# Four-layer graph network: GpSimd takes part of layer 0's last products, and pass 1's closing is written in fewer operations

## The chip, the cores and the metric

The kernel runs on one core of a Trainium2 chip. The metric is the device time in microseconds, the median over several executions. One further execution was recorded by the hardware profiler; all rows below are from it.

## The reference, cut to what matters

```python
edge_index = stack([src, dst])                       # 100000 edges sorted by dst, 6250 nodes, 256 features
x = layernorm(x + L0(x, edge_index))                 # GAT, 8 heads of 32
x = layernorm(x + L1(x, edge_index))                 # two GCN convolutions, 256 -> 512 -> 256
x = layernorm(x + L2(x, edge_weight, src, dst))
x = layernorm(x + L3(x, edge_index, edge_attr_2))
...
# L0, for each edge: the row of its source times a weight for each head, summed over dst
e = leaky_relu(a_src[src] + a_dst[dst], 0.2); e_exp = exp(e - e_max[dst])
out = segment_sum(h[src] * e_exp[:, :, None]) / denom; out = relu(out + bias)
...
# L1
h = relu(layer_norm(gcn_conv(x, W1, b1), gamma1, beta1))   # layer_norm: (h - mu) * rsqrt(var + eps) * gamma + beta
g = relu(layer_norm(gcn_conv(h, W2, b2), gamma2, beta2))
```

## The kernel before

The 6250 nodes lie in 49 tiles of 128. The edges, sorted by destination, are worked through in steps of at most 128 edges of one tile. For each step GpSimd starts an indirect DMA that gathers the source rows, TensorE multiplies them by a one-hot matrix of destinations, and VectorE adds the product to the tile's sums (`reg_acc`). When a tile has all its steps, its closing follows, spread over the steps behind: `closing(i)` in layer 0 and `closings(i)` in the passes say which tile is in which part `n` at step `i`. All orders are written out by hand, engine by engine, and each engine works its program in order. A wait is a `wait_ge` on a semaphore.

**Layer 0** (`heads_*`) has 832 steps in 52 groups of 16; the groups 50 and 51 are the last. `heads_gpsimd` issues the 832 gathers (L1031), then waits for all of them and copies the shifted edge indices into `src_idx` (L1037) for the passes. A gathered row must be multiplied by its eight weights before TensorE can use it. `heads_vector` does that for step `i` ("weigh", L1354), then a part of the next group's scores (`chain_vector`), then `add(i - 3)` (L1337), then the part of the closing. The weights of a group come from ScalarE (L1114) at the end of the group before, after VectorE's `below` (L1276). The wait in `add` for the add before it makes adds follow one another. TensorE waits for `weighted0(i)` in order of `i`. L943 to L972 are a tile's closing on VectorE, L992 to L1000 that on ScalarE. Afterwards the last normed tile is stored, and GpSimd begins pass 1.

**Pass 1** is the first half of L1 and what lies between its two convolutions, 783 gathers. `pass1_vector` closes a tile in these parts: scale and bias out of PSUM (L1563, n = 5), moments (L1567, L1569), reciprocal of the root, subtract and scale (L1572, L1574, n = 8), gamma (L1577), beta (L1580). `pass1_scalar` makes the root (L1539), the relu (L1543, n = 11), and the copies of turned tiles out of PSUM (`Dense.keep`, L165; TensorE's `turn` and `multiply` are L157 and L172). GpSimd begins pass 2 (`e.wait_ge(*h2_stored.end)`) when the last tile's result (L1548) is stored. Passes 2 and 3 are built alike. In pass 2, L1714 and L1722 are gamma and beta over 256 columns. L2114 and L2130, in layer 3's closing, are an addition on GpSimd and a multiplication on VectorE over seven tiles at once.

Of the kernel before, what the change touches and what calls it, by code (L numbers as in the profile page):

```python
# [13 lines left out]
P = 128  # L14
# [125 lines left out]
class Dense:  # L140
# [20 lines left out]
    def keep(self, e, j):  # L161
        e.wait_ge(*self.turned(j))
        if j >= 2:
            e.wait_ge(*self.product(j - 2))
        e.copy(self.ring[:, j % 2, :], self.turn_bank(j)[:, 0:self.k_chunks * P]).then_inc(*self.kept.up)  # L165
# [94 lines left out]
def build(nc, io):  # L260
    ctx = ExitStack()
    with ctx:
# [84 lines left out]
        s_chain = {n: signal(f"{n}_chain") for n in ("vector", "tensor", "scalar")}  # L347
        s_far, s_hot4 = signal("distance_made"), signal("four_hots_made")
# [3 lines left out]
        s_cleared, s_hidden = signal("sums_cleared"), signal("hidden_made")  # L352
# [659 lines left out]
        weighted0 = s_weighted.take(STEPS_PAD)  # L1012
        product0, added0 = s_edge.take(STEPS_PAD), s_added.take(STEPS_PAD)
        scaled0, denscaled0 = s_scaled.take(GROUPS - 1), s_denscaled.take(GROUPS - 1)

# [6 lines left out]
        def heads_gpsimd(e):  # L1022
# [11 lines left out]
            for k in range(3):  # L1034
                e.wait_ge(*got0[k].end)
            e.wait_ge(*h0_v.at("src_at"))
# [280 lines left out]
        def heads_vector(e):  # L1317
# [31 lines left out]
            for i in range(STEPS_PAD):  # L1349
                g, k = i // S, i % S  # L1350
                row = rows0[:, i % (3 * S), :]
                v = row[:, 0:FEAT].rearrange("p (h d) -> p h d", h=H)
                e.wait_ge(*ch_a.at("weights", g))
                e.tensor_tensor(v, v, bcast(row[:, FEAT:ROW0], 2, [P, H, D]), ALU.mult).then_inc(*weighted0.up)  # L1354
# [125 lines left out]
        def closings(i):  # L1480
# [16 lines left out]
        stat1, moment1, inverse1, shift1, gamma1_done, beta1_done = (  # L1497
            s.take(NODE_TILES) for s in (norm_a[0], norm_a[1], norm_a[3], norm_a[4], s_gamma, s_beta))
        root1, hidden = s_hid_in.take(NODE_TILES), s_hidden.take(NODE_TILES)
# [13 lines left out]
        def pass1_tensor(e):  # L1513
            e.wait_ge(*loads1.end)
            for i in range(RANKED + PARTS):
                if i < RANKED:
                    edges1.step(e, i)
                for k, n in closings(i):
# [3 lines left out]
                    if n == 4:  # L1522
                        dense1.multiply(e, k, taken1)
                    if n == 12:
                        e.wait_ge(*hidden(k))
                        dense2.turn(e, k)
                    if n == 14:
                        dense2.multiply(e, k, taken2)

        def pass1_scalar(e):  # L1530
            edges1.hots(e, range(8))
            for i in range(RANKED + PARTS):
                edges1.hots_ahead(e, i)
                for k, n in closings(i):
# [5 lines left out]
                    if n == 11:  # L1540
                        h = hid[:, k % 4, :]
                        e.wait_ge(*beta1_done(k))
                        e.activation(h, h, ACT.Relu).then_inc(*hidden.up)  # L1543
                    if n == 13:
                        dense2.keep(e, k)
                    if n == 16:
# [719 lines left out]
```

## Time and profile before

| | |
|---|---|
| median of 3 runs | 5286.16 us (5281.18 to 5288.01) |
| profiled execution | 5284.91 us, its span 5283.1 us |
| TensorE's granted clock, mean | 0.824 of full speed |
| busy in the span | PE 74%, VectorE (DVE) 66%, ScalarE (ACT) 49%, GpSimd (POOL) 73% |
| layer 0's steps | to about 1209 us |
| pass 1, pass 2, pass 3, layer 3 | from 1216, 2226, 3223 and 4213 us |

The span runs from the first to the last instruction. Busy shares are means over stages with different limits.

### The profile page before, as it was taken

The numbers are of one execution on the slowest core, as the hardware profiler recorded it, in microseconds if no ns is written. First come the engines' busy times: TensorE is split into PE (matmuls) and PEld (weight loads), VectorE is DVE, ScalarE is ACT, GpSimd is POOL, SyncE is SP. The second block draws the span as 40 slices with busy tenths as digits, with TensorE's granted clock in tenths as the row PEclk, the third lists the DMA queues.
The fourth block names the chain that finished last, engine by engine and source line by source line (L and its number), as shares of the span: only waits on it lengthen the run. The fifth ranks groups of instructions, "written<-read, shape, count | busy, mean of one in ns | idle before, by whom it ended". The sixth has DMA issues, their size and how long they took to land.

```text
span 5283.1 us, 86663 instructions
## 1 busy us (share of the span) xinstructions
PE 3888.6 (74%) x13357; PEld 2393.2 (45%) x13357; DVE 3504.2 (66%) x10780; ACT 2567.7 (49%) x6941; POOL 3861.1 (73%) x3995
## 2 busy tenths in 40 slices
PE   7888888886777777677777777676777657666663
PEld 5666666663444444344434434343334334444442
DVE  5889888885555455354444445666666578888887
ACT  3667666674555555355555551000000166666665
POOL 3777777766777777677777776777777777777775
PEclk8889889898998999777787787878887777777776
DMA  6444444433333333443333333333333322222222
GB/s 171 117 123 123 123 122 122 124 108 106 110 112 111 112 111 112 127 133 112 113 112 111 112 112 100 109 109 109 109 110 109 97 57 57 57 57 57 57 57 67
DMA packets 252627, 549.14 MB, mean 104 GB/s; under 512 B 71467, under 2 KB 136235, under 8 KB 252108
## 3 DMA queue, kind: packets, MB, share of 16 engines
q0 software_dynamic: 178752, 478.34, 33.3%
q1 hardware_dynamic: 45804, 42.37, 2.6%
q10 hardware_dynamic: 27552, 22.89, 1.5%
q8 instruction: 157, 2.57, 0.2%
q14 instruction: 362, 2.97, 0.2%
HBM read 501.16 MB, written 42.15 MB: 103 GB/s over the span
## 4 chain that ended last, share of the span: by engine, by line
POOL 55%; issue 20%; PE 10%; ACT 6%; DVE 4%; DMA 2%; SPq 1%; DVEq 0%; ACTq 0%; POOLq 0%
POOL scratch L1416 41%; POOL scratch L1886 14%; PE bank L1312 5%; PE bank L1161 3%; ACT scratch L1073 2%; DMA scratch<-tab_x,src_idx 1%; DVE reg_acc L1337 1%; PE bank L1149 1%; ACT scratch L1085 1%; DVE reg_x L1354 1%; SPq L872 1%; ACT scratch L1076 1%; DMA scratch<-tab_h,src_idx 1%; POOL reg_x L1031 0%; ACT scratch L1121 0%
## 5 line engine op out<-in xcount | busy, mean ns | idle before, releaser
L1468 PE MATMUL bank<-scratch 128*128 x4986 | 1904.2, 495 | 761.6 <-SPq L1428 407.3
L1478 DVE TENSOR_TENSOR reg_acc<-reg_acc,bank 128x256 f32 x2493 | 1048.1, 420 | 1361.7 <-PE bank L1468 1298.4
L1416 POOL DMA_INDIRECT scratch<-tab_x,src_idx x1566 | 1491.5, 952 | 533.3 <-issue 469.4
L1468 PEld LDWEIGHTS bank<-scratch 128*128 128x128 f32 x4986 | 964.3, 228 | 1602.9 <-issue 1549.0
L1031 POOL DMA_INDIRECT reg_x<-tab_h,src_idx x832 | 831.6, 1000 | 291.0 <-issue 176.7
L1416 POOL DMA_INDIRECT scratch<-tab_h,src_idx x783 | 744.4, 951 | 260.7 <-issue 234.3
L1886 POOL DMA_INDIRECT scratch<-tab_h,src_idx x783 | 741.2, 947 | 248.6 <-issue 237.7
L1937 PE MATMUL bank<-reg_w,scratch 128*128 128x260 f32 x1664 | 637.5, 527 | 286.6 <-issue 185.2
L1437 ACT ACTIVATE scratch<-iota_row,dst_loc 128x128 f32<-128x128 f32 x1662 | 572.1, 392 | 348.2 <-PE bank L1468 333.9
L1312 PE MATMUL bank<-reg_x,scratch 128*128 128x265 f32 x1664 | 577.8, 458 | 73.3 <-DVE reg_x L1354 71.1
L1937 PEld LDWEIGHTS bank<-reg_w,scratch 128*128 128x128 f32 x1664 | 377.3, 253 | 509.7 <-issue 312.1
L1968 ACT ACTIVATE edge_w<-scratch,attr 128x68 f32 x832 | 288.5, 347 | 311.1 <-SPq L1898 281.9
L1312 PEld LDWEIGHTS bank<-reg_x,scratch 128*128 128x128 f32 x1664 | 302.9, 215 | 203.6 <-DVE reg_x L1354 172.1
L1337 DVE TENSOR_TENSOR reg_acc<-reg_acc,bank 128x265 f32 x832 | 355.3, 427 | 45.8 <-PE bank L1312 35.3
L2054 DVE TENSOR_TENSOR reg_acc<-reg_acc,bank 128x260 f32 x832 | 350.3, 421 | 16.1 <-PE bank L1937 3.6
L1354 DVE TENSOR_TENSOR reg_x<-reg_x 128x256 f32<-128x256 f32 x832 | 344.6, 414 | 0.5 <-ACT reg_x L1114 0.5
L1453 DVE TENSOR_SCALAR scratch<-iota_row,dst_loc,edge_w 128x128 f32<-128x128 f32 x831 | 322.3, 389 | 6.1 <-issue 6.1
L1952 ACT ACTIVATE scratch<-iota_row,dst_loc 128x128 f32<-128x128 f32 x832 | 319.8, 386 | 3.4 <-DMA tab_h<-reg_w 1.6
L1787 ACT ACTIVATE adst<-adst,small 128x1 f32<-128x1 f32 x49 | 14.4, 294 | 611.2 <-DVE adst L1830 611.2
L2037 DVE SCALAR_TENSOR_TENSOR reg_w<-scratch,attr,edge_w 128x68 f32<-128x68 f32 x832 | 237.8, 286 | 95.0 <-ACT edge_w L1968 83.4
L2085 DVE TENSOR_TENSOR reg_w<-reg_w,bank 128x520 f32<-128x520 f32 x416 | 286.2, 688 | 0.5
L1442 ACT ACTIVATE scratch<-scratch 128x512 f32<-128x512 f32 x416 | 261.7, 629 | 13.1
(314 smaller groups left out, 4374.9 us busy)
## 6 DMA issues: line engine op xcount, KB each, us to landing
scratch<-tab_x,src_idx POOLq DMA_INDIRECT x1566, 2.8
scratch<-tab_h,src_idx POOLq DMA_INDIRECT x1566, 2.7
reg_x<-tab_h,src_idx POOLq DMA_INDIRECT x832
tab_h<-scratch ACTq DMA_DIRECT2D x7, 924.0 KB, 6.4
reg_x<-in_x SPq DMA_DIRECT2D x7, 896.0 KB, 11.3
reg_w<-in_x SPq DMA_DIRECT2D x49, 128.0 KB, 2.5
tab_x<-reg_acc SPq DMA_DIRECT2D x49, 128.0 KB
tab_xs<-reg_w SPq DMA_DIRECT2D x49, 128.0 KB, 2.7
```

Of the source, the lines that this page charges most:

```text
L1031: e.indirect_dma_start(rows0[:, t % (3 * S), 0:ROW0], None, tab_h0, bass.IndirectOffsetOnAxis(ap=src_idx[:, t:t + 1], axis=0)).then_inc(*g ...
L1312: e.matmul(psum[i % BANKS0][:, 0:W0_ROW], hots0[:, i % (2 * S), :], rows0[:, i % (3 * S), :], start=True, stop=True).then_inc(*product0.up)
L1337: e.tensor_tensor(v, v, psum[i % BANKS0][:, 0:W0_ROW], ALU.add).then_inc(*added0.up)
L1354: e.tensor_tensor(v, v, bcast(row[:, FEAT:ROW0], 2, [P, H, D]), ALU.mult).then_inc(*weighted0.up)
L1416: e.indirect_dma_start(ring_rows[:, j % SLOTS, :], None, self.table, bass.IndirectOffsetOnAxis(ap=src_idx[:, j:j + 1], axis=0)).then_inc(* ...
L1437: e.activation(ring_hots[:, i % HOTS, :], iota_row[:, :], ACT.Abs, scale=-1.0, bias=dst_loc[:, i:i + 1]).then_inc(*self.far.up)
L1453: e.tensor_scalar(ring_hots[:, i % HOTS, :], iota_row[:, :], dst_loc[:, i:i + 1], edge_w[:, i:i + 1], ALU.is_equal, ALU.mult).then_inc(*se ...
L1468: e.matmul(self.bank(i), ring_hots[:, i % HOTS, :], rows, start=True, stop=True).then_inc(*self.product.up)
L1478: e.tensor_tensor(v, v, self.bank(i), ALU.add).then_inc(*self.added.up)
L1886: e.indirect_dma_start(ring_rows[:, j % SLOTS, 0:ROW3], None, tab_h3, bass.IndirectOffsetOnAxis(ap=src_idx[:, j:j + 1], axis=0)).then_inc( ...
L1937: e.matmul(psum[i % BANKS][:, 0:WIDE3], hots3[:, i % HOTS, :], scaled3[:, i % 4, :], start=True, stop=True).then_inc(*product3.up)
L2054: e.tensor_tensor(v, v, psum[i % BANKS][:, 0:WIDE3], ALU.add).then_inc(*added3.up)
```

## The change

In layer 0, `BY_POOL` holds the even steps of the last two groups, 16 steps. GpSimd multiplies their rows, behind its last gather and ahead of the copy of `src_idx`; VectorE skips them. In pass 1, (h - mean) * gamma is one `scalar_tensor_tensor`, made beside the root, and (that) * inverse + beta a second one; the relu is taken in the activation that copies the turned tile out of PSUM. `keep` is an `activation` everywhere now, with the function Copy by default.

```diff
-    def keep(self, e, j):
+    def keep(self, e, j, act=ACT.Copy):
...
-        e.copy(self.ring[:, j % 2, :], self.turn_bank(j)[:, 0:self.k_chunks * P]).then_inc(*self.kept.up)
+        e.activation(self.ring[:, j % 2, :], self.turn_bank(j)[:, 0:self.k_chunks * P], act).then_inc(*self.kept.up)
...
-        weighted0 = s_weighted.take(STEPS_PAD)
+        BY_POOL = [i for i in range(STEPS_PAD - 2 * S, STEPS_PAD) if i % 2 == 0]
+        weighted_v = s_weighted.take(STEPS_PAD - len(BY_POOL))
+        weighted_p = s_pool_weighted.take(len(BY_POOL))
...
+        def weighted0(i):
+            return weighted_p(BY_POOL.index(i)) if i in BY_POOL else weighted_v(i - sum(n < i for n in BY_POOL))
+
+        def weigh(e, i):
+            row = rows0[:, i % (3 * S), :]
+            v = row[:, 0:FEAT].rearrange("p (h d) -> p h d", h=H)
+            return e.tensor_tensor(v, v, bcast(row[:, FEAT:ROW0], 2, [P, H, D]), ALU.mult)
...
             for k in range(3):
                 e.wait_ge(*got0[k].end)
+            for i in BY_POOL:
+                e.wait_ge(*ch_a.at("weights", i // S))
+                weigh(e, i).then_inc(*weighted_p.up)
             e.wait_ge(*h0_v.at("src_at"))
             e.tensor_copy(src_idx[:, 0:POSITIONS], src_at_i).then_inc(*h0_p.done("src_idx"))
...
-                e.wait_ge(*ch_a.at("weights", g))
-                e.tensor_tensor(v, v, bcast(row[:, FEAT:ROW0], 2, [P, H, D]), ALU.mult).then_inc(*weighted0.up)
+                if i not in BY_POOL:
+                    e.wait_ge(*ch_a.at("weights", g))
+                    weigh(e, i).then_inc(*weighted_v.up)
...
-                    if n == 12:
-                        e.wait_ge(*hidden(k))
-                        dense2.turn(e, k)
-                    if n == 14:
+                    if n == 10:
+                        e.wait_ge(*beta1_done(k))
+                        dense2.turn(e, k)
+                    if n == 12:
                         dense2.multiply(e, k, taken2)
...
                     if n == 11:
-                        h = hid[:, k % 4, :]
-                        e.wait_ge(*beta1_done(k))
-                        e.activation(h, h, ACT.Relu).then_inc(*hidden.up)
-                    if n == 13:
-                        dense2.keep(e, k)
-                    if n == 16:
+                        dense2.keep(e, k, ACT.Relu)
+                    if n == 14:
...
+                    if n == 7:
+                        e.wait_ge(*moment1(k))
+                        e.scalar_tensor_tensor(out=h, in0=h, scalar=cells_a.mean(k), in1=gamma1, op0=ALU.subtract,
+                                               op1=ALU.mult).then_inc(*gamma1_done.up)
                     if n == 8:
                         e.wait_ge(*root1(k))
                         e.reciprocal(root, root).then_inc(*inverse1.up)
+                    if n == 9:
                         e.wait_ge(*inverse1(k))
-                        e.tensor_scalar(h, h, cells_a.mean(k), root, ALU.subtract, ALU.mult).then_inc(*shift1.up)
-                    if n == 9:
-                        e.wait_ge(*shift1(k))
-                        e.tensor_tensor(h, h, gamma1, ALU.mult).then_inc(*gamma1_done.up)
-                    if n == 10:
                         e.wait_ge(*gamma1_done(k))
-                        e.tensor_tensor(h, h, beta1, ALU.add).then_inc(*beta1_done.up)
+                        e.scalar_tensor_tensor(out=h, in0=h, scalar=root, in1=beta1, op0=ALU.mult,
+                                               op1=ALU.add).then_inc(*beta1_done.up)
```

The order of GpSimd's instructions behind layer 0's gathers, before:

```order
L1031 DMA reg_x<-tab_h,src_idx 128x264 x832
L1037 COPY src_idx<-reg_w 128x783
L1416 DMA scratch<-tab_x,src_idx 128x256 x783
L1416 DMA scratch<-tab_h,src_idx 128x256 x783
L1416 DMA scratch<-tab_x,src_idx 128x256 x783
L1886 DMA scratch<-tab_h,src_idx 128x136 x783
```

and of the change:

```order
L1042 DMA reg_x<-tab_h,src_idx 128x264 x832
L1025 TENSOR_TENSOR reg_x<-reg_x 128x256 x16
L1051 COPY src_idx<-reg_w 128x783
L1429 DMA scratch<-tab_x,src_idx 128x256 x783
L1429 DMA scratch<-tab_h,src_idx 128x256 x783
L1429 DMA scratch<-tab_x,src_idx 128x256 x783
```

The sixteen multiplications stand between the gathers of layer 0 and the copy.

VectorE amid group 51, before (L1354 is a weigh, L1337 an add, L962 and L966 are the closing of a tile; ISA is a wait):

```order
L1337 TENSOR_TENSOR reg_acc<-reg_acc,bank 128x265
L962 SCALAR_TENSOR_TENSOR reg_w<-reg_acc,reg_w 128x256
L1354 TENSOR_TENSOR reg_x<-reg_x 128x256
L877 ISA
L1337 TENSOR_TENSOR reg_acc<-reg_acc,bank 128x265
L966 BN_STATS small<-reg_w 128x6
L1354 TENSOR_TENSOR reg_x<-reg_x 128x256
L877 ISA
L1337 TENSOR_TENSOR reg_acc<-reg_acc,bank 128x265
```

and of the change, where L1025 is a weigh and L1351 an add:

```order
L1351 TENSOR_TENSOR reg_acc<-reg_acc,bank 128x265
L963 SCALAR_TENSOR_TENSOR reg_w<-reg_acc,reg_w 128x256
L1025 TENSOR_TENSOR reg_x<-reg_x 128x256
L878 ISA
L1351 TENSOR_TENSOR reg_acc<-reg_acc,bank 128x265
L967 BN_STATS small<-reg_w 128x6
L878 ISA
L1351 TENSOR_TENSOR reg_acc<-reg_acc,bank 128x265
L970 BN_AGGR small<-small 128x2
```

Between stats and the add behind them the weigh is gone.

VectorE at the last tile's closing in pass 1, before (`adst` holds the moments and the root, `reg_x` the hidden rows, `reg_w` bias, gamma and beta):

```order
L1563 SCALAR_TENSOR_TENSOR reg_x<-bank,dinv,reg_w 128x512
L1567 BN_STATS adst<-reg_x 128x6
L1569 BN_AGGR adst<-adst 128x2
L1572 RECIPROCAL adst<-adst 128x1
L1574 TENSOR_SCALAR reg_x<-reg_x,adst 128x512
L1577 TENSOR_TENSOR reg_x<-reg_x,reg_w 128x512
L1580 TENSOR_TENSOR reg_x<-reg_x,reg_w 128x512
```

and of the change:

```order
L1572 SCALAR_TENSOR_TENSOR reg_x<-bank,dinv,reg_w 128x512
L1576 BN_STATS adst<-reg_x 128x6
L1578 BN_AGGR adst<-adst 128x2
L1581 SCALAR_TENSOR_TENSOR reg_x<-reg_x,adst,reg_w 128x512
L1585 RECIPROCAL adst<-adst 128x1
L1589 SCALAR_TENSOR_TENSOR reg_x<-reg_x,adst,reg_w 128x512
```

Gamma moved ahead of the reciprocal, and three wide operations behind the moments became two.

## Rows read from the trace of the kernel before

**Rows 1.** The page: the chain that ended last, by engine

```profile
POOL 55%; issue 20%; PE 10%; ACT 6%; DVE 4%; DMA 2%; SPq 1%; DVEq 0%; ACTq 0%; POOLq 0%
```

**Rows 2.** Busy us by stretch: length, PE, PEld, DVE, ACT, POOL, clock, DMA share, GB/s

```profile
1216.00:2203.00 987.00, 762.86 (x2514) 445.47 (x2515) 494.70 (x1163) 509.19 (x1276) 748.74 (x783) 0.91 0.39 113
```

**Rows 3.** Timeline of GpSimd: start, us, operation, [idle before, releaser]

```profile
1172.10 0.92 POOL L1037 COPY src_idx<-reg_w 128x783 int32<-128x783 int32 x1 [2.55 <-DMA reg_x<-tab_h,src_idx]
1216.02 0.98 POOL L1416 DMA_INDIRECT scratch<-tab_x,src_idx  x1 [43.01 <-DMA tab_x<-reg_acc]
```

**Rows 4.** Timeline of VectorE: one operation in groups 49 and 50

```profile
1172.23 0.81 DVE L1273 TENSOR_SCALAR scratch<-scratch 128x8 f32<-128x8 f32 x1
...
1191.45 0.17 DVE L1273 TENSOR_SCALAR scratch<-scratch 128x8 f32<-128x8 f32 x1
```

**Rows 5.** Timeline of VectorE in group 51

```profile
1199.46 0.42 DVE L966 BATCH_NORM_STATS2 small<-reg_w 128x6 f32<-128x256 f32 x1
1199.79 0.41 DVE L1354 TENSOR_TENSOR reg_x<-reg_x 128x256 f32<-128x256 f32 x1
...
1207.83 0.43 DVE L1337 TENSOR_TENSOR reg_acc<-reg_acc,bank 128x265 f32 x1 [0.22 <-DVE reg_acc L1337]
```

**Rows 6.** Timeline of ScalarE in group 50

```profile
1177.50 0.48 ACT L1121 COPY scratch<-bank 128x384 f32<-128x384 f32 x1 [1.12 <-PE bank L1170]
...
1186.89 0.16 ACT L1102 COPY scratch<-bank 128x2 f32<-128x2 f32 x1
...
1192.52 0.32 ACT L1114 ACTIVATE reg_x<-scratch 128x128 f32<-128x128 f32 x1 [2.92 <-DVE scratch L1276]
```

**Rows 7.** Timeline of GpSimd in layer 3's closing

```profile
5230.81 5.43 POOL L2114 TENSOR_TENSOR reg_x<-reg_acc,reg_x 128x1792 f32<-128x1792 f32 x1
...
5258.05 3.65 POOL L2114 TENSOR_TENSOR reg_x<-reg_acc,reg_x 128x1792 f32<-128x1792 f32 x1
```

**Rows 8.** Timeline of VectorE in layer 3's closing

```profile
5227.27 5.46 DVE L2130 TENSOR_TENSOR reg_acc<-reg_acc,edge_w 128x1792 f32<-128x1792 f32 x1
```

**Rows 9.** Timeline of GpSimd in pass 1, three of its longest gathers

```profile
1272.32 1.42 POOL L1416 DMA_INDIRECT scratch<-tab_x,src_idx  x1 [0.30 <-issue]
1291.56 1.37 POOL L1416 DMA_INDIRECT scratch<-tab_x,src_idx  x1 [0.30 <-issue]
...
2200.02 1.37 POOL L1416 DMA_INDIRECT scratch<-tab_x,src_idx  x1 [0.30 <-issue]
```

**Rows 10.** Timeline of VectorE beside the second of them

```profile
1291.42 0.68 DVE L1580 TENSOR_TENSOR reg_x<-reg_x,reg_w 128x512 f32<-128x512 f32 x1
```

**Rows 11.** The chain in order of time, tail of pass 1: start, us, what

```profile
2213.01 0.30 ACT adst L1539
...
2213.34 0.18 DVE adst L1572
...
2213.54 0.56 DVE reg_x L1574
...
2214.12 0.70 DVE reg_x L1577
...
2214.85 0.70 DVE reg_x L1580
...
2215.57 0.64 ACT reg_x L1543
...
2216.26 1.13 PE bank L157 x4
```

**Rows 12.** Groups of VectorE in pass 1 and pass 2: busy us, mean ns | idle before

```profile
L1563 DVE SCALAR_TENSOR_TENSOR reg_x<-bank,dinv,reg_w 128x512 f32<-128x512 f32 x49 | 36.5, 745 | 4.0 <-PE bank L172 4.0
...
L1714 DVE SCALAR_TENSOR_TENSOR reg_acc<-reg_acc,adst,reg_w 128x256 f32<-128x256 f32 x49 | 23.6, 481 | 0.0
```

**Rows 13.** Group of ScalarE in pass 1: the keep of 512 columns

```profile
L165 ACT COPY reg_x<-bank 128x512 f32<-128x512 f32 x49 | 28.3, 578 | 34.8 <-PE bank L157 34.7
```

**Rows 14.** The line of the gathers in pass 1: ns min, median, max

```profile
L1416 POOL DMA_INDIRECT scratch<-tab_x,src_idx x783: 942/946/1451, 1216.0 to 2202.9; - x196
```

More of the change, by code:

```diff
@@ L347, in build @@
         s_chain = {n: signal(f"{n}_chain") for n in ("vector", "tensor", "scalar")}
+        s_pool_weighted = signal("rows_weighted_by_gpsimd")
         s_far, s_hot4 = signal("distance_made"), signal("four_hots_made")
@@ L351, in build @@
         s_degree, s_gamma, s_beta = signal("degree_scaled"), signal("gamma_scaled"), signal("beta_added")
-        s_cleared, s_hidden = signal("sums_cleared"), signal("hidden_made")
+        s_cleared = signal("sums_cleared")
         s_hid_in, s_hid_v = signal("hidden_root"), signal("hidden_normed")
@@ L1350, in heads_vector @@
                 g, k = i // S, i % S
-                row = rows0[:, i % (3 * S), :]
-                v = row[:, 0:FEAT].rearrange("p (h d) -> p h d", h=H)
-                e.wait_ge(*ch_a.at("weights", g))
-                e.tensor_tensor(v, v, bcast(row[:, FEAT:ROW0], 2, [P, H, D]), ALU.mult).then_inc(*weighted0.up)
+                if i not in BY_POOL:
+                    e.wait_ge(*ch_a.at("weights", g))
+                    weigh(e, i).then_inc(*weighted_v.up)
                 if g + 1 < GROUPS:
@@ L1496, in build @@
         taken1, taken2 = s_taken.take(NODE_TILES), s_taken2.take(NODE_TILES)
-        stat1, moment1, inverse1, shift1, gamma1_done, beta1_done = (
-            s.take(NODE_TILES) for s in (norm_a[0], norm_a[1], norm_a[3], norm_a[4], s_gamma, s_beta))
-        root1, hidden = s_hid_in.take(NODE_TILES), s_hidden.take(NODE_TILES)
+        stat1, moment1, inverse1, gamma1_done, beta1_done = (
+            s.take(NODE_TILES) for s in (norm_a[0], norm_a[1], norm_a[3], s_gamma, s_beta))
+        root1 = s_hid_in.take(NODE_TILES)
         h2_stored = s_store.take(T)
```

## The prediction

> **What bounds the kernel now.** I read the page's chain first. GpSimd has 55% of it and "issue" 20% [rows 1]. Both are one thing: GpSimd makes the descriptors of a gather in about 0.95 us and starts the next 0.30 us later. From 1216 to 2203 us GpSimd runs 783 gathers, 748.74 us busy, while PE, VectorE and ScalarE are at 77%, 50% and 52% [rows 2]. So in pass 1 work taken from VectorE or ScalarE is worth nothing as such. Only three kinds of place can move the end: where GpSimd has nothing to issue (before 1216 us it sat idle 43.01 us until the last tile of layer 0 was stored [rows 3]); the serial tail of pass 1 behind the last gather; and whatever makes one gather longer than its 0.95 us. The timeline was read next for the end of layer 0, then the chain for the tail, then the gathers' durations.
>
> **Part 1a, the tail of pass 1.** After the last gather one tile goes through its closing alone, and the chain names every step [rows 11]: root 2213.01 (0.30), reciprocal 2213.34 (0.18), subtract and scale 2213.54 (0.56), gamma 2214.12 (0.70), beta 2214.85 (0.70), relu 2215.57 (0.64), TensorE's turn at 2216.26. Pass 2's first gather waits for what follows. In the new order gamma comes first, needs only the moments, and so starts at 2213.01 beside the root. Its form, scalar_tensor_tensor with a pointer scalar over 512 columns, stands in the trace at 745 ns (its first input from PSUM), and at 256 columns with both inputs in SBUF at 481 ns [rows 12]. I take 0.745: done 2213.76. The root (0.30) is done by then. Reciprocal: in pass 2, whose code has this form already, it adds about 0.10 behind such an operation, so 2213.86. With 0.02 of hand-over the second fused operation runs 2213.88 to 2214.62, and the turn starts with 0.05 more at 2214.67, against 2216.26: **-1.6 us**. Bounds: -1.8 if each takes 0.68 like gamma and beta, -1.3 if the reciprocal waits its full 0.18 and each takes 0.80.
>
> **Part 1b, the copies.** Every dense keep was a COPY (578 ns at 512 columns [rows 13]) and is now an activation. The nearest activation of 512 columns is the relu that is removed, 0.64 in [rows 11]. Some 0.05 each; in serial places stand two in pass 1's tail and one in pass 3's: **+0.15 us** (0 to +0.3). The other keeps lie under the gathers.
>
> **Part 1c, the gathers of pass 1.** Against the median of 946 ns [rows 14], 748.74 us for 783 gathers is 8.0 us too much. The long ones come about once a tile; 42 lie above 0.97 us, the first and the last are in [rows 9]. The one of 1291.56 took 1.37 with beta, begun at 1291.42, over its start [rows 9, 10]. I set all 42 beside VectorE's timeline: 16 begin under beta (their excess over 0.95 adds up to 5.2 us), 15 under gamma (2.35), 11 under the subtract and scale (1.5). A gather that begins while such an operation runs ends as late as the operation lets it start; L1563, with one input in PSUM, never does that in 49 tiles. So two of the three culprits go or change: three operations become two, both with two SBUF inputs. Each fused one follows a step with little behind it, as gamma did in most tiles, while beta came on a backlog of three wide operations. I price each like gamma, raised by (0.56/0.50) squared for its longer hold: 2.9 us, together 5.9 against 9.0: **-3.1 us**. Bounds: -8 if no gather is hit any more, +4 if both fall like beta (2 x 5.2 x 1.25 = 13).
>
> The Trainium skill (SBUF — State Buffer, Who interferes with whom) has a VectorE instruction with two SBUF inputs contend with GpSimd instructions that read SBUF, and infers that a tensor_tensor leaves descriptor generation alone. The trace shows otherwise for beta, by the 1.37 us. By that inference all the excess would belong to the subtract and scale and would go.
>
> **Part 2, the end of layer 0.** Sixteen multiplications of 128x256 leave VectorE and go to GpSimd, behind its last gather and ahead of the copy of src_idx. VectorE paces these stretches, at one weigh and one add a step.
> - *The copy moves.* It ran at 1172.10 for 0.92 [rows 3] and VectorE's L1273, issued under it, took 0.81 instead of 0.17 [rows 4]; that is on the chain. Gone here: -0.64. It comes back behind the multiplications, amid group 51, and blocks one operation by up to 0.9: +0.4.
> - *Price of one multiplication on GpSimd.* Nearest rows: 128x1792 took 3.65 undisturbed, the last of its seven [rows 7]. With 0.1 fixed, 256 columns give 0.61, of which some 0.55 hold what VectorE also needs. That it is held exclusively, turn by turn, shows in layer 3's residual at the program's end: VectorE's multiplication issued at 5227.27 took 5.46 instead of 2.0, ended at 5232.7, and GpSimd's, begun at 5230.81, took 5.43 instead of 3.65 [rows 7, 8].
> - *Group 50.* ScalarE works without a gap that VectorE decides from 1177.50 to 1187.05 [rows 6], so eight weighs saved and eight turns lost there stay hidden: 0. Without that cover the eight blocks cost up to 8 x 0.3 = 2.4 less the 2.7 of the saved weighs. Only the weigh of step 814 stands between the last scores and the weights of group 51: -0.34.
> - *Group 51* (from 1192.84 [rows 6]). Before, a step was 0.67: weigh 0.34 and add 0.34. Two adds in a row cannot be nearer than 0.65, since each waits 0.22 for the last [rows 5]. A weigh that goes saves 0.33 only where another operation fills its place, as stats at 1199.46 in front of the weigh of 1199.79 [rows 5]: two such and three half ones, -1.0. Against it: a pair of steps needs VectorE's weigh after two of GpSimd's turns (2 x 0.55 + 0.05 + 0.34 = 1.49 instead of 1.34), four pairs: +0.6, and the five or six closing operations with two SBUF inputs wait some 0.3 each: +1.7. Net +1.3; with turns of 0.45, +0.6; with 1.0, +4.3.
> Sum: -0.64 + 0.4 - 0.34 + 1.3 = **+0.7 us**, bounds -1.5 and +6. GpSimd is done near 1200 us, long before 1216.02 [rows 3]. The first product of group 51 is not later than before: GpSimd starts it with the weights, while VectorE had an add in hand.
>
> **Sum.** -1.6 + 0.15 - 3.1 + 0.7 = -3.85 us. On the profiled execution's 5284.91 that is 5281.1; on the median of the three runs, 5286.16, it is **5282.3 us**. The profiled one lies 1.25 under the median, inside the runs' own spread of 6.8. A change of 0.2% (10.6 us) is about what a measurement of this kernel can tell from none. So the forecast is: no measurable change.
>
> **Rivals.**
> 1. *Gathers free (the skill's inference).* If only the subtract and scale held the gathers up, -8.0 replaces -3.1: 5277.4. Against it: [rows 9, 10], and 31 of 42. Chance 0.08.
> 2. *GpSimd's multiplication is dear.* Its operands here are 8 blocks of 32 columns with a broadcast factor, a shape that the trace lacks. At 1.0 us each, layer 0 loses 3.7 instead of 0.7: 5285.3. Chance 0.12.
> 3. *Slower.* The same mechanism at its far end: the eighth product of group 51 (row 830) is ready at 1192 + 8X, and its add stood at 1207.83 [rows 5], its matmul 1 us ahead. From X = 1.85 us on GpSimd paces the end. To lose 10.6 us over the whole it must cost 15.2 here: X = 3.75, about what the whole 128x1792 operation takes. 5296.8 or more. Chance 0.03.
> 4. *Faster by more than 0.2%.* All stalls gone (-8), the tail -1.8, layer 0 at its lower bound -1.5: -11.3, 5274.9. All three bounds at once: 0.05.
> 5. *Nothing from part 2.* The group-50 saving is hidden and group 51 even: 5281.6; not to be told from the forecast.
> The forecast with its own range (5278 to 5288) has 0.72.
>
> **Chances and range.** Rivals 1, 2 and the forecast lie within 0.2%: 0.92; faster 0.05; slower 0.03. The range takes rivals 1 and 2, the stall term's +4 and a spread of 3 us between runs: 5275 to 5290.
>
> **What would show it.** In the tail: gamma's row beside the root's, and some 1.6 us less from moments to turn. In pass 1: busy time of the 783 gathers near 746 us, no gather long under an operation with an input in PSUM. At 1172: L1273's successor at 0.17. In group 51: sixteen GpSimd rows of 0.6, the first eight within 10 us, VectorE's two-input rows stretched to 0.6 to 0.9, and the stretch from the weights to the last add some 1.3 longer. I would be wrong if the multiplications took over 1 us, if the stalls fell in a fixed bad phase (13 us or more), or if the hand-over of 1216 moved by more than 2 us either way.

## The result: 39 us slower, outside the predicted range

In alternating runs on one chip the changed kernel took 5326.63 us in the median (5326.12 to 5332.12), the kernel before 5287.09 (5281.18 to 5292.37): a ratio of **1.0077, with a 95% interval of 1.006 to 1.0095**. 5282.3 us had been predicted, 5275 to 5290.

The chain of the kernel after, by engine, reads as that of [rows 1] did, to the percent or nearly:

```profile
POOL 55%; issue 20%; PE 10%; ACT 5%; DVE 4%; DMA 3%; SPq 0%; DVEq 0%; ACTq 0%; POOLq 0%
```

No new wait and no new bound shows in it. The busy time of the engines in pass 1 of the kernel after (the columns are those of [rows 2]) says more:

```profile
1217.50:2221.00 1003.50, 764.69 (x2518) 448.11 (x2519) 474.14 (x1114) 489.61 (x1229) 764.93 (x783) 0.92 0.39 111
```

VectorE and ScalarE have 20 us less to do each, as meant. But the 783 gathers keep GpSimd busy for 764.93 us, against 748.74. The stretches of the profiled executions, from first gather to first gather and so on, give the whole difference (spans 5283.1 and 5324.4 us):

| stretch | before | after | difference |
|---|---|---|---|
| start to pass 1's first gather | 1216.0 | 1217.5 | +1.5 |
| pass 1, first to last gather | 986.9 | 1002.4 | +15.4 |
| tail of pass 1, to pass 2's first gather | 23.4 | 21.2 | -2.2 |
| pass 2, first to last gather | 981.7 | 991.0 | +9.4 |
| pass 3, the same | 979.2 | 987.7 | +8.5 |
| layer 3, the same | 978.5 | 987.1 | +8.6 |
| the two hand-overs between, and the end | 117.4 | 117.6 | +0.2 |

Passes 2 and 3 and layer 3 have not one changed instruction of GpSimd, and lose 26 us of the 41. The line of the gathers shows how: one stretch after another of the kernel after, duration in ns as minimum/median/maximum, then first and last start:

```profile
L1042 POOL DMA_INDIRECT reg_x<-tab_h,src_idx x832: 949/954/1686, 85.5 to 1171.7; - x167
L1429 POOL DMA_INDIRECT scratch<-tab_x,src_idx x783: 952/957/1482, 1217.5 to 2219.9; - x196
L1896 POOL DMA_INDIRECT scratch<-tab_h,src_idx x783: 951/955/1169, 4246.1 to 5233.2; - x196
```

and the first and the last of these lines in the kernel before (the middle one is in [rows 14], 942/946/1451):

```profile
L1031 POOL DMA_INDIRECT reg_x<-tab_h,src_idx x832: 942/947/2046, 84.7 to 1168.3; - x167
L1886 POOL DMA_INDIRECT scratch<-tab_h,src_idx x783: 938/944/1194, 4213.1 to 5191.7; - x196
```

The gathers have become 7 to 13 ns longer, in the minimum as well as in the median. That is 1% of a gather, and there are 3964 of them in layer 0, the passes and layer 3, issued back to back. It holds for layer 0's gathers too, which begin at 85 us, long before the first of the sixteen multiplications runs at 1174.79. Even the seven small gathers of the preparation (`reg_acc<-in_edge_floats`, from 30 us on) take 954 ns in the mean against 945. So it is no collision with what the change executes nearby. Three times 782 pitches that are 11 to 12 ns longer make the 26.5 us of the last three passes. In pass 1 the same 11 ns give 8.6 us of the 15.4; the other 6.7 or so are longer stalls, treated below.

What the sixteen multiplications cost GpSimd itself is as forecast. The timeline of GpSimd in the kernel after, behind its last gather of layer 0 (consecutive ones are joined, "x8"):

```profile
1174.79 5.86 POOL L1025 TENSOR_TENSOR reg_x<-reg_x 128x256 f32<-128x256 f32 x8 [2.08 <-DMA reg_x<-tab_h,src_idx]
1192.94 5.38 POOL L1025 TENSOR_TENSOR reg_x<-reg_x 128x256 f32<-128x256 f32 x8 [12.28 <-ACT reg_x L1128]
1198.27 1.03 POOL L1051 COPY src_idx<-reg_w 128x783 int32<-128x783 int32 x1
1217.52 1.02 POOL L1429 DMA_INDIRECT scratch<-tab_x,src_idx  x1 [18.22 <-DMA tab_x<-reg_acc]
```

and its line (minimum, median, maximum):

```profile
L1025 POOL TENSOR_TENSOR reg_x<-reg_x x16: 612/792/827, 1174.8 to 1197.5; 128x256 f32<-128x256 f32 x16
```

### The profile page after: what moved, and what is told of

The parts are those of the page before. It is cut to its first block, busy times and chain, and to the rows that moved or that the text cites. A ratio compares the mean times of both kernels' runs of the same rounds, so it can differ in the third digit from the quotient of the medians.

```text
span 5324.4 us, 86614 instructions
## 1 busy us (share of the span) xinstructions
PE 3917.3 (74%) x13357; PEld 2397.2 (45%) x13357; DVE 3474.2 (65%) x10715; ACT 2552.6 (48%) x6892; POOL 3915.5 (74%) x4011
## 4 chain that ended last, share of the span: by engine, by line
POOL 55%; issue 20%; PE 10%; ACT 5%; DVE 4%; DMA 3%; SPq 0%; DVEq 0%; ACTq 0%; POOLq 0%
POOL scratch L1429 41%; POOL scratch L1896 14%; PE bank L1326 5%; PE bank L1175 3%; ACT scratch L1087 2%; PE bank L1163 1%; DVE reg_acc L1351 1%; ACT scratch L1099 1%; DMA scratch<-tab_h,src_idx 1%; DMA reg_x<-tab_h,src_idx 1%; DMA scratch<-tab_x,src_idx 1%; DVE reg_x L1025 1%; POOL reg_x L1042 1%; ACT scratch L1090 1%; SPq L873 0%
## 5 line engine op out<-in xcount | busy, mean ns | idle before, releaser
L1429 POOL DMA_INDIRECT scratch<-tab_x,src_idx x1566 | 1515.2, 968 | 508.9 <-issue 472.8
L1429 POOL DMA_INDIRECT scratch<-tab_h,src_idx x783 | 753.6, 962 | 258.6 <-issue 235.3
L1896 POOL DMA_INDIRECT scratch<-tab_h,src_idx x783 | 749.8, 958 | 248.7 <-issue 236.4
L1351 DVE TENSOR_TENSOR reg_acc<-reg_acc,bank 128x265 f32 x832 | 353.1, 424 | 35.2 <-PE bank L1326 22.9
L1025 DVE TENSOR_TENSOR reg_x<-reg_x 128x256 f32<-128x256 f32 x816 | 337.0, 413 | 0.5 <-ACT reg_x L1128 0.5
L1466 DVE TENSOR_SCALAR scratch<-iota_row,dst_loc,edge_w 128x128 f32<-128x128 f32 x831 | 308.6, 372 | 6.1 <-issue 6.1
```

What stands on the lines that cost most here:

```text
L1025: return e.tensor_tensor(v, v, bcast(row[:, FEAT:ROW0], 2, [P, H, D]), ALU.mult)
L1351: e.tensor_tensor(v, v, psum[i % BANKS0][:, 0:W0_ROW], ALU.add).then_inc(*added0.up)
L1429: e.indirect_dma_start(ring_rows[:, j % SLOTS, :], None, self.table, bass.IndirectOffsetOnAxis(ap=src_idx[:, j:j + 1], axis=0)).then_inc(* ...
L1896: e.indirect_dma_start(ring_rows[:, j % SLOTS, 0:ROW3], None, tab_h3, bass.IndirectOffsetOnAxis(ap=src_idx[:, j:j + 1], axis=0)).then_inc( ...
```

## Experiments

**A remark on the chips.** The groups of runs fell on different chips, and on three of them the same kernel before takes 6669 to 6765 us: there GpSimd's gathers last as long as elsewhere but are not what bounds. The page of such a run (`e3_one_semaphore`, the kernel before but for one unused semaphore) has this chain, and this group of the gathers, before which GpSimd waited 463 us for SyncE's queue:

```profile
PE 43%; issue 26%; another core or an unknown queue 8%; DVE 8%; ACT 7%; DVEq 3%; ACTq 2%; SPq 1%; POOL 1%; DMA 0%; POOLq 0%
...
L1417 POOL DMA_INDIRECT scratch<-tab_x,src_idx x1566 | 1492.8, 953 | 1005.9 <-SPq L1427 463.2
```

So of those runs I use the durations of the gathers, which can be compared across chips, and their times only against the kernel before on the same chip.

| run | gathers, median ns | time, us | before there, us |
|---|---|---|---|
| e1_pass1_only | 946 | 6608.5, ratio 0.9876 [0.9852, 0.9901] | 6683.9 |
| e2_gpsimd_only | 960 | 6671.5, 0.9978 [0.9956, 1.0001] | 6683.9 |
| e3_one_semaphore | 946 | 6682.5, 1.0001 [0.9982, 1.0021] | 6683.9 |
| e4_after_again | 957 | 6596.7, 0.9859 [0.9819, 0.9899] | 6683.9 |
| e5_pass1_only_again | 946 | 5286.3, 1.0002 [0.9992, 1.0012] | 5283.5 |
| f1_one_product | 957 | 5326.1 | 5283.5 |
| f2_sixteen_memsets | 946 | 5280.0 | 5283.5 |
| f3_sixteen_plain | 957 | 5327.1 | 5283.5 |
| g1_sixteen_adds | 960 | 6666.5 | 6669.1 |
| g2_no_gpsimd_add | 946 | 6679.7, 1.002 [0.9998, 1.0041] | 6669.1 |
| g3_no_gpsimd_copy | 946 | 6670.1 | 6669.1 |
| g4_second_later | 949 | 6654.3, 0.997 [0.9946, 0.9995] | 6669.1 |
| h1_products_no_copy | 946 | 5297.8, 1.0001 [0.9987, 1.0015] | 5297.9 |
| h2_behind_copy | 946 | 5291.9 | 5297.9 |
| h3_behind_gathers | 949 | 5298.9 | 5297.9 |
| h4_after_moved | 960 | 5331.9 | 5297.9 |
| i1_copy_first | 957 | 6696.3, 0.9904 [0.988, 0.9929] | 6764.7 |
| i2_product_first | 946 | 6771.0 | 6764.7 |

Times without a ratio are single executions; those of the kernel before on one chip differ among themselves by up to 29 us (5287.4 to 5316.3 beside h1), so a single time can show the loss of 34 us or more that is at stake here, and nothing finer. The median is that of the passes' first line (passes 1 and 3). Two groups stand apart: 946 to 949, and 957 to 960.

### Which part of the change does it

Theory A: the work on GpSimd lengthens the gathers. Rival: the new semaphore, or pass 1's new order. The changed kernel without the multiplications:

```diff
-        BY_POOL = [i for i in range(STEPS_PAD - 2 * S, STEPS_PAD) if i % 2 == 0]
+        BY_POOL = []
```

> The changed kernel with an empty BY_POOL: VectorE weighs every row, the rest as changed. Theory A (something fixed that comes with the sixteen products in GpSimd's program makes each of 3181 later or earlier gathers 10 us/1000 longer, 957 ns instead of 946, some 34 us in all): median of a gather back at 946 ns, pass 1's stalls stay at 15.7 us against 9.1, so about 5287 + 6.7 - 2.3 = 5291 us. Theory B (it comes with pass 1's new closing, or with the activation that replaces COPY): gathers at 957 ns, about 5325 us. Theory C (the chip or the session, not the program): gathers like those of the kernel before on the same chip, whichever they are.

The kernel before with the multiplications alone (the diff's parts in `heads_gpsimd` and `heads_vector`):

> The kernel before with only the sixteen products on GpSimd. Theory A: gathers at 957 ns in every stage, also before the products run, about 5287 + 34 + 0 to 1.5 = 5321 to 5323 us. Theory B: 946 ns, 5287 to 5289 us. Theory C: ratio to before 1.000.

The kernel before with one semaphore more, which nothing uses:

```diff
+        s_pool_weighted = signal("rows_weighted_by_gpsimd")
```

> The kernel before with one more semaphore, never used, allocated where the change allocates its own: all semaphores behind it move by one number, nothing else changes. If the 10 ns come from semaphore numbers or from mere placement (theory D): gathers at 957 ns or another value than 946, 5290 to 5325 us. Theories A, B and C: ratio 1.000 within 0.1%, gathers at 946 ns.

And the changed kernel once more:

> The changed kernel once more, beside the kernel before on this chip. Theories A, B and D: ratio 1.0077 again, 957 ns a gather. Theory C: another ratio, near 1.000 to 1.002.

946, 960, 946 and 957 ns: the multiplications on GpSimd alone lengthen the gathers; pass 1's part and a semaphore don't. Since GpSimd doesn't bound on this chip, the longer gathers cost nothing here (e2: 0.9978), and pass 1's part gains 1.2%: from pass 1's first gather to pass 2's it takes 1243 us in e1, against 1315 in e3. The first run was therefore repeated on a chip like that of the result:

> Pass 1's part alone once more, hoping for a chip on which the kernel before takes 5287 us as in the comparison, not 6684 us. There the gathers were 946 ns in e1 and 957 ns wherever the sixteen products are in GpSimd's program. Theory A (all of the 34 us hang on those 10 ns a gather): 946 ns, and 5287 - 2.3 (tail) + 6.7 (stalls) = 5291 us, ratio 1.0008. Theory B (pass 1's closing costs more on this chip): over 1.003.

1.0002: where the gathers bound, pass 1's part alone neither gains nor loses, and the gathers are as before:

```profile
L1429 POOL DMA_INDIRECT scratch<-tab_x,src_idx x783: 942/946/1473, 1224.1 to 2217.8; - x196
```

### How many, and what kind of instruction

One multiplication (step 800) instead of sixteen:

```diff
-        BY_POOL = [i for i in range(STEPS_PAD - 2 * S, STEPS_PAD) if i % 2 == 0]
+        BY_POOL = [STEPS_PAD - 2 * S]
```

> The changed kernel with one single row (step 800) given to GpSimd. Theory A1 (the number of GpSimd instructions, or the shift of those behind them, decides): 946 ns or something between. Theory A2 (that such an operation is there at all): 957 ns in every stage, like sixteen.

In the kernel before, ahead of the copy of `src_idx`, sixteen memsets of a tile that nothing else uses; and, in another run, one memset and sixteen products of that tile (and, in a further run, sums):

```diff
+            for _ in range(16):
+                e.memset(dead[:, :], 0.0).then_inc(*dead_n.up)
+                e.wait_ge(*dead_n(_))
```

> The kernel before, with sixteen memsets of 128x256 into an unused tile on GpSimd where the products would stand. Theory A1 (sixteen more instructions of any kind): 957 ns a gather. Theory A2 (the kind: a two-input operation with three-dimensional operands): 946 ns. Output unchanged.

```diff
+            e.memset(dead[:, :], 0.0).then_inc(*dead_n.up)
+            for n in range(16):
+                e.wait_ge(*dead_n(n))
+                e.tensor_tensor(dead[:, :], dead[:, :], dead[:, :], ALU.mult).then_inc(*dead_n.up)
```

> The kernel before, with one memset and sixteen plain 128x256 multiplications of an unused tile with itself on GpSimd in that place, two dimensions and no broadcast. Theory A1: 957 ns. Theory A2 in its narrow form (the broadcast shape): 946 ns; in its wide form (a multiplication on GpSimd, where before there was only layer 3's addition): 957 ns.

> As f3_sixteen_plain (957 ns a gather, 5327 us), but the sixteen plain operations on GpSimd are additions. Theory M (a multiplication in GpSimd's program is what lengthens the gathers, since the kernel before has already seven additions there, in layer 3's closing, at 946 ns): 946 ns, about 5284 us. Theory S (any two-input operation ahead of or amid the gathers, the seven additions being behind them all): 957 ns, about 5326 us.

The lines of the gathers of f1, f2 and f3, in this order:

```profile
L1429 POOL DMA_INDIRECT scratch<-tab_x,src_idx x1566: 952/957/1474, 1221.3 to 4235.4; - x196
```

```profile
L1421 POOL DMA_INDIRECT scratch<-tab_x,src_idx x1566: 942/946/1426, 1211.1 to 4195.4; - x196
```

```profile
L1422 POOL DMA_INDIRECT scratch<-tab_x,src_idx x1566: 951/957/1452, 1224.0 to 4234.6; - x196
```

One multiplication lengthens the gathers as much as sixteen, and with it the time is 5326.1 us. f3 leaves the change out altogether and is as slow, 5327.1 us: 35 us of that lie between the first and the last gather of the four stages, and another 8 in a later start of pass 1 (1224.0 us), a moment that varies between runs, as said below. Neither the operands (a broadcast factor or a plain tile) nor the operation matter (g1), but a memset does nothing. So what counts is that a two-input instruction (TENSOR_TENSOR) stands there in GpSimd's program, and not the amount of work.

### Is it where the instruction stands

The kernel before has seven such instructions too, behind all gathers (L2114), without harm. In one run VectorE made those additions instead; in another, with the additions back on GpSimd, VectorE made the copy:

> The kernel before with layer 3's seven residual additions on VectorE, so that GpSimd's program holds no two-input operation at all. Theory K (each kind of operation in GpSimd's program costs each gather some ns): the median falls below 946 ns, by up to 10 ns, and the kernel gains up to 3181 x 0.01 = 32 us, less some 10 us that the closing loses because VectorE makes the additions itself. Theory M alone: 946 ns, and 0 to +13 us for the closing.

> The kernel before with the copy of src_idx on VectorE, behind the last gather's landing and the last steps of layer 0. Theory K: the median falls below 946 ns. Theory M: 946 ns, and the hand-over at 1216 us is later by up to 1 us.

946 ns in both: taking either off GpSimd doesn't shorten the gathers. Four runs then moved things. In the first, the whole change stays and VectorE makes the copy:

```diff
         def heads_gpsimd(e):
...
-            e.wait_ge(*h0_v.at("src_at"))
-            e.tensor_copy(src_idx[:, 0:POSITIONS], src_at_i).then_inc(*h0_p.done("src_idx"))
...
         def close0_vector(e):
+            for k in range(3):
+                e.wait_ge(*got0[k].end)
+            e.wait_ge(*h0_v.at("src_at"))
+            e.tensor_copy(src_idx[:, 0:POSITIONS], src_at_i).then_inc(*h0_p.done("src_idx"))
```

> The changed kernel with the copy of the source indices done by VectorE, so that GpSimd has no COPY left beside its 16 products. If what lengthens the gathers is the order in which GpSimd's instruction kinds first come (a two-input one ahead of the COPY), the gathers' median is back at 946 ns against 957, and, on a chip where the gathers bound the kernel, the time at 1.000 of before. If it is two-input instructions amid the gathers wherever they stand, 957 ns and 1.0075. Where the sequencers bound instead, the gathers' median decides alone.

The next two are f3 with its sixteen products moved. In the first they stand behind the copy, while the memset stays ahead of it; in the second the memset and the products stand behind all gathers:

> The kernel before with 16 products of a tile of zeros put behind the copy of the source indices and ahead of pass 1's gathers (the same 16 ahead of the copy gave 957 ns). Order of first use: the gathers are at 946 ns. Two-input instructions amid the gathers: 957 ns.

> The kernel before with the same 16 products put behind all the gathers, just ahead of layer 3's additions. Both order of first use and position amid the gathers say 946 ns, and a few us more at the end of the program. If it is only that the program is longer or laid out otherwise, the gathers differ from 946 ns.

The last is the changed kernel with an unused semaphore allocated ahead of the others:

> The changed kernel with one unused semaphore allocated ahead of the others, so that all the others have another number. Order and position say 957 ns as in the changed kernel. If the numbers of the semaphores or the placement of the program carry it, another value, 946 ns at the lowest.

The lines of h1, h2, h3 and h4:

```profile
L1431 POOL DMA_INDIRECT scratch<-tab_x,src_idx x1566: 942/946/1462, 1213.8 to 4201.4; - x196
```

```profile
L1422 POOL DMA_INDIRECT scratch<-tab_x,src_idx x1566: 942/946/1382, 1223.1 to 4209.6; - x196
```

```profile
L1418 POOL DMA_INDIRECT scratch<-tab_x,src_idx x1566: 945/949/1464, 1214.6 to 4211.0; - x196
```

```profile
L1430 POOL DMA_INDIRECT scratch<-tab_x,src_idx x1566: 954/960/1477, 1219.1 to 4238.8; - x196
```

h2 holds the same instructions as f3, only with the products behind the copy, and its gathers are at 946 ns instead of 957. h1 shows that GpSimd can do all sixteen multiplications amid the gathers without harm, if no copy follows them. That struck out the position amid the gathers, and left, I thought, the order in which GpSimd's kinds of instruction come first: a TENSOR_TENSOR ahead of the COPY is slow. h4's 3 ns, and h3's, show a second, smaller thing that goes with a program as a whole.

Two runs tested that order. The changed kernel with a tiny COPY at the very start:

```diff
         def prep_gpsimd(e):
+            e.memset(dead[:, 0:1], 0.0).then_inc(*dead_n.up)
+            e.wait_ge(*dead_n(0))
+            e.tensor_copy(dead[:, 1:2].bitcast(I32), dead[:, 0:1].bitcast(I32)).then_inc(*dead_n.up)
```

> The changed kernel, all of it, with a COPY of 128x1 int32 on GpSimd at the very start, ahead of all gathers, so that a COPY comes in GpSimd's program before a two-input operation. If the order of first use carries the lengthening, the gathers' median goes from 957 ns back to 946 (949 by placement) and the time, where the gathers bound the kernel, to 0.999 to 1.001 of before. If it doesn't, 957 ns and 1.0075.

and the kernel before with a tiny multiplication there:

```diff
+            e.memset(dead[:, 0:1], 0.0).then_inc(*dead_n.up)
+            e.wait_ge(*dead_n(0))
+            e.tensor_tensor(dead[:, 1:2], dead[:, 0:1], dead[:, 0:1], ALU.mult).then_inc(*dead_n.up)
```

> The kernel before with one multiplication of 128x1 elements on GpSimd at the very start, 85 us ahead of layer 0's gathers, and its copy of the indices where it was. If it is the order of first use, the gathers take 957 ns although nothing else differs, and the time is 34 us longer. If a two-input operation has to stand amid the gathers, 946 ns and the time of before.

The two as they ran, at the start of GpSimd's timeline (i1 first), each with the line of its gathers:

```profile
0.92 0.18 POOL L475 COPY dead<-dead 128x1 int32<-128x1 int32 x1
...
L1434 POOL DMA_INDIRECT scratch<-tab_x,src_idx x1566: 951/957/1436, 1540.6 to 5168.1; - x196
```

```profile
0.93 0.19 POOL L474 TENSOR_TENSOR dead<-dead 128x1 f32<-128x1 f32 x1
...
L1421 POOL DMA_INDIRECT scratch<-tab_x,src_idx x1566: 940/946/1422, 1532.7 to 5248.2; - x196
```

Both came out against the theory: with the COPY first the gathers stay at 957, with the multiplication first they stay at 946. Order of first use is refuted.

**What stays.** All seven programs with a two-input instruction directly ahead of the copy of `src_idx`, behind layer 0's gathers (the changed kernel, e2, f1, f3, g1, h4, i1), have gathers of 957 or 960 ns. All eleven others, the kernel before among them, have 946 or 949: those with the two in the other order (h2), with the copy gone (h1), and with a two-input instruction far ahead of the copy (i2). It goes with the program and not with the chip: the changed kernel has 957 ns on two chips (e4 is the second), pass 1's part alone 946 on two (e1 and e5). Why it reaches gathers that are issued over a millisecond earlier isn't settled: something that is fixed with the program, such as where its instructions lie, or something that one execution leaves to the next. No run told these two apart. And with 949 and 960 about, which no order of instructions explains, seven against eleven programs is a pattern and not a mechanism.

### The stalls in pass 1

In e5, where the gathers have their old median, they are still busy 6.9 us longer in pass 1 than before (756.5 us for the 783, against 749.6), through long single ones. The timeline of the kernel after shows two, on GpSimd and on VectorE:

```profile
1250.37 1.26 POOL L1429 DMA_INDIRECT scratch<-tab_x,src_idx  x1 [0.30 <-issue]
1251.94 1.32 POOL L1429 DMA_INDIRECT scratch<-tab_x,src_idx  x1 [0.30 <-issue]
```

```profile
1250.06 0.74 DVE L1581 SCALAR_TENSOR_TENSOR reg_x<-reg_x,adst,reg_w 128x512 f32<-128x512 f32 x1
...
1251.69 0.75 DVE L1589 SCALAR_TENSOR_TENSOR reg_x<-reg_x,adst,reg_w 128x512 f32<-128x512 f32 x1
```

Each of the two gathers starts 0.25 to 0.3 us into one of the fused operations and takes 0.3 to 0.4 us longer. Set beside VectorE's timeline as in the prediction, the excess of the long gathers over the median adds up to:

| | long gathers | under the first | the second | the third | sum |
|---|---|---|---|---|---|
| before (L1574, L1577, L1580) | 42 | 1.5 us | 2.4 | 5.2 | 9.1 us |
| after (L1581, L1589) | 50 | 7.5 | 8.2 | | 15.7 |
| h1_products_no_copy | 42 | 5.4 | 7.5 | | 12.9 |

The sum isn't fixed by the code, though. Taken over all 783 gathers of pass 1 (their busy time less 783 medians), it is 8.9, 8.2, 9.9, 9.2 and 12.8 us in five profiles with the old closing (before, f2, h2, f3, h3), and 15.6, 15.8, 12.6, 12.6 and 14.1 in five with the new one (after, e5, f1, h1, h4), all on chips where the gathers bound. The two sets all but touch. The new closing costs 4.3 us more in the mean of these, and the 6.7 between the two profiles of the result contain some chance.

What decides for a single gather shows when each is sorted by how far into the fused operation it starts (kernel after, L1581 and L1589 together):

| starts into the operation | gathers | excess over the median |
|---|---|---|
| under 0.09 us | 12 | none |
| 0.09 to 0.2 | 14 | 0.43 to 0.53 us |
| 0.2 to 0.3 | 15 | 0.32 to 0.38 |
| 0.3 to 0.4 | 9 | 0.25 to 0.33 |
| 0.4 to 0.6 | 11 | 0.09 to 0.21 |
| over 0.6 | 11 | none |

So a gather that starts some 0.1 to 0.6 us into the operation ends about as late as if it had started 0.62 us into it; one that starts earlier or later loses nothing. The start decides, and neither the number nor the width of the operations alone.

Whether another order of parts would shift the starts to a better place is a further question. One run put the second fused operation and all parts behind it one step later (turn 11, keep 12, multiply 13, the last product 15), without the multiplications on GpSimd:

```diff
-                    if n == 9:
+                    if n == 10:
                         e.wait_ge(*inverse1(k))
```

> Pass 1's part alone (as e1 and e5), with the second fused operation a step later (part 10 instead of 9, what follows moved alike). In e5 the gathers of pass 1 were 15.6 us over their median, 31 of the 50 long ones under the second fused operation, since it falls mostly 0.7 to 1.2 us behind a gather's start. Theory P (the place in the 1.25 us cadence of the gathers decides): another excess, 5 to 20 us, above all for the second operation. Theory N (the number and width of two-input operations decides): again 15 to 16 us. Median of a gather 946 ns in both; total 5280 to 5292 us.

It ran on a chip where GpSimd doesn't bound: 24 long gathers, 6.3 us. But e1, whose parts are where the change has them, has only 27 and 5.2 us on such a chip, against 52 and 16.2 for the same program in e5: the pace there is another, and 20 of the gathers under its fused operations start in the harmless first 0.09 us, against 11 in e5. The run therefore says nothing on what the new order is worth where the gathers bound. That stays untested.

## Why the prediction was wrong, step by step

**What bounds: right in substance, wrong in what followed from it.** "GpSimd makes the descriptors of a gather in about 0.95 us and starts the next 0.30 us later" holds. I took the 0.95 as given, and listed as a place that can move the end "whatever makes one gather longer than its 0.95 us", meaning collisions. That the program itself sets the 0.946 or 0.957 had no term in the sum and no rival. That is the step that failed, a term put at nothing without a reason: the change was taken to leave the length of all gathers outside pass 1's collisions as it was. Instead, 11 ns for each of the 3132 gathers of the passes and layer 3 make some 34 us of the 41 in the span (946 against 957 ns in the two profiles; the 7 ns of layer 0's 832 are mostly not on the path). It was not to be read from the trace of before, which has one value for it; but a chain with 55% of one instruction repeated 3964 times would have justified asking what 1% of it costs, before pricing parts to 0.1 us.

**Part 1a, the tail: right.** The chain of the kernel after, in order of time, answers to [rows 11]:

```profile
2229.49 0.75 DVE reg_x L1581
2230.24 0.09 DVE adst L1585
...
2230.35 0.76 DVE reg_x L1589
...
2231.15 1.13 PE bank L157 x4
2232.28 0.02 issue
2232.30 0.61 ACT reg_x L165
```

From gamma's start to the turn it is 1.66 us; from the root's start it was 3.25. That is -1.6, as predicted, and 0.745 per fused operation and 0.10 for the reciprocal are right to 0.02. The whole tail is 2.2 us shorter. The rest comes from steps ahead of the closing, which the change leaves alone: TensorE's product in front of it (L172) takes 2.00 us on the chain instead of 3.07, while the last steps before it take longer.

**Part 1b, the copies: smaller than thought.** ScalarE's keeps took 373 ns as COPY and take 384 as activation at 256 columns, 587 and 598 at most: 0.01 us each, not 0.05. The bound of 0 to +0.3 us for the three holds.

**Part 1c, the stalls: the sign was wrong.** -3.1 had been predicted, with +4 as the bound; it is +6.7 (15.7 against 9.1), and +3.8 in h1. Pricing the fused operations "like gamma" was the error: gamma's excess was 2.4 us and beta's 5.2, and the fused ones have 7.5 and 8.2. 49 of the 50 long gathers start under one of the two. Over five profiles of either closing it is +4.3 in the mean, and none of the five with the new one comes near the 6 us that the forecast gave it (the lowest has 12.6). So the sign is clearly wrong, and only the size of the loss is uncertain. The "13 us or more" that was named as a sign of being wrong was reached in the result, but not through "a fixed bad phase": the starts fall all over the operation, as the table above shows.

**Part 2, the end of layer 0: right in its prices, not to be told in its sum.** The multiplication costs GpSimd 0.61 us at the least, the price taken from the 128x1792 row, and 0.79 in the median; VectorE was at work beside all sixteen. From the start of group 51's weights to that of the last add it is 17.4 us in the kernel after and 17.1 in h1, against 16.0 before: +1.5 and +1.1, where +1.3 was predicted. But it is 15.3 in e5, where VectorE weighs all rows as before, so half of this is within what the stretch varies by. The stretch ahead of it, from group 50's weights to group 51's, is 20.6 us in the kernel after and 17.8 in h1; without multiplications on GpSimd it was 18.6 (before), 18.5 (e5) and 20.2 (h3). VectorE's small operation before the weights of group 50 is back at 0.16 us, since the copy has gone from there [rows 4], and amid group 51 its own products are stretched, both as said. The first line is from VectorE's timeline of the kernel after, the second from its groups between 1190 and 1200 us:

```profile
1170.87 0.16 DVE L1287 TENSOR_SCALAR scratch<-scratch 128x8 f32<-128x8 f32 x1
...
L1025 DVE TENSOR_TENSOR reg_x<-reg_x 128x256 f32<-128x256 f32 x4 | 2.5, 629 | 0.0
```

The first gather of pass 1 came 1.5 us later, in h1 2.2 earlier; in kernels whose layer 0 works as before this moment differs by more than that (1214.6 in h3, 1216.0 before, 1224.1 in e5), so the sum of Part 2, +0.7, can't be confirmed or refuted by these profiles.

**The rivals.** Gathers free: refuted, L1581 and L1589 hold them up. The multiplication dear, or slow from 3.75 us each: refuted by 0.61 to 0.83. "Slower" had only this mechanism and 0.03; the kernel became slower by another, so even that chance was given for a wrong reason. "Faster" asked for all stalls to go, and they grew. "Nothing from part 2" can't be told from the forecast, as it said itself.

**What the change would be without the surprise.** h1, all of the change with the copy on VectorE, is at 1.0001 [0.9987, 1.0015]; its profiled span is 5282.6 us against 5283.1. That is the "no measurable change" of the forecast, but only in part for the reasons given there: the stalls, at +3.8 where -3.1 stood, eat what the tail gains. That the two roughly cancel is luck. No version measurably faster than before was found on such a chip.

## What to carry to other kernels

Where one instruction is repeated back to back thousands of times on the path, first compare its median duration in both traces: here a hundredth of it outweighed every local saving, and it can change in stages that the edit doesn't touch. An instruction of a kind that an engine had not run at that place is a risk of its own, however short; if the gathers get longer, move it past its neighbours (h2) or give the neighbour to another engine (h1), and measure again. A VectorE operation of 128x512 with two inputs in SBUF lengthens a gather that starts 0.1 to 0.6 us into it, so fewer but longer ones are not a gain unless their starts keep out of that stretch.

## What the runs showed of the hardware

- The same gather on GpSimd lasts 946 or 957 ns (median; 949 and 960 also occur), for the whole program. All seven programs with a TENSOR_TENSOR directly ahead of the COPY behind layer 0's gathers have the longer one, and none of eleven others. One such instruction is enough (f1); sixteen memsets do nothing (f2), nor does a TENSOR_TENSOR at the very start (i2). The cause is open. The time went up by 34 to 44 us where the gathers bound (the result, f1, f3, h4), and not at all where they don't (e2).
- A gather that starts 0.09 to 0.6 us into a scalar_tensor_tensor of 128x512 with two SBUF inputs takes longer, by about 0.62 us less that start: up to 0.5 us more (maximum 1.48, median 0.957). The 23 that start earlier or later in it lose nothing, nor do the 20 that start under the one with an input in PSUM (L1572).
- GpSimd multiplies 128x256 f32 in 0.61 us at the least and 0.79 in the median beside a busy VectorE, whose own products of this size then take 0.63 us in the mean instead of 0.42 (four of them between 1190 and 1200 us).
- The kernel before takes 5284 to 5298 us in the median on some chips and 6669 to 6765 on others, with gathers of the same length. On the slower ones the edit of pass 1 gains 1.2% (e1); on the faster ones it gains nothing (e5, 1.0002).
